# Feed-forward turns of a decoder kernel: where the square, the gelus, the table loads and the down projection stand

## The reference, cut to what matters

```
for i in range(6):
    x = attn_layer(shift_tokens(x), ...) + x
    x = ffn_layer(shift_tokens(x), ...) + x

attn_layer:  q, k, v = x @ Wqkv          # 16 heads of 64
             q, k = l2norm(q) * qs, l2norm(k) * ksc ; rotate both
             softmax(8 * q @ k.T, window of 32 and the one before) @ v @ Wo
ffn_layer:   xn = (x - mean) / sqrt(var + 1e-5) * g + bln
             a, gate = split(xn @ W1 + b1)                # 341 each
             (a * gelu(gate)) @ W2 + b2
```

## Time and profile before

| | before |
|---|---|
| runs (median, lowest, highest) | 1274.28 us, 1273.89, 1277.31 |
| the profiled execution | 1272.33 us, span of its trace 1270.5 us |
| the stack: first square sum L1680, last down pass L1375 | 397.8 us, 1254.7 us of the span |
| PE / DVE / ACT / POOL busy, whole span | 90% / 75% / 67% / 51% |
| head-norm square sum L1680 on POOL | 96 times, 1287 ns |
| squares L1426 on ACT | 192 times, 596 ns |
| square of the centred stream L1502 on ACT | 12 times, 613 ns |
| down projection L1375 on PE | 72 passes, 592 ns |
| table loads L1473, L1511, L1514 | 24, 12, 12 times, 1283 ns each |
| granted TensorE clock, 550 to 752 us | 1.00 of full speed |

### The profile page before, as it was taken

One profiled execution on the slowest core, in us unless ns is written; L12 is line 12 of the kernel. 1 busy time (PEld: TensorE's weight loads), 2 busy tenths in 40 slices (PEclk: granted clock), 3 DMA queues, 4 the chain that ended last, 5 costly groups with the idle time before them and its releaser, 6 DMA issues. The chain is left out here.

```text
span 1270.5 us, 26317 instructions
## 1 busy us (share of the span) xinstructions
PE 1138.3 (90%) x9636; PEld 720.2 (57%) x9636; DVE 949.0 (75%) x1399; ACT 847.5 (67%) x1356; POOL 650.1 (51%) x522
## 2 busy tenths in 40 slices
PE   7787869999765899999999999999999999999976
PEld 2222337777422576666656676666666666667541
DVE  2789957777465778787878788877878787878733
ACT  4553536665335588777877788678877787777844
POOL 1555723444323675664657465655566465756510
PEclk9888979999786899999999999999999999999997
DMA  3000007110200454344525453435434453534310
GB/s 113 1 1 0 1 17 217 51 50 1 77 24 19 97 155 99 93 123 107 133 74 129 103 134 88 112 102 134 99 98 123 109 126 76 126 90 120 87 49 17
DMA packets 75510, 107.11 MB, mean 84 GB/s; under 512 B 25347, under 2 KB 31938, under 8 KB 75002
## 3 DMA queue, kind: packets, MB, share of 16 engines
q1 hardware_dynamic: 75386, 105.47, 31.9%
HBM read 30.89 MB, written 0.59 MB: 25 GB/s over the span
## 5 line engine op out<-in xcount | busy, mean ns | idle before, releaser
L1680 POOL TENSOR_TENSOR st_sq_sum<-h 128x512 f32<-128x512 f32 x96 | 123.5, 1287 | 250.0 <-ACT h L1426 249.4
L1563 DVE SCALAR_TENSOR_TENSOR st_turned<-banks,mo_w 128x1024 f32<-128x1024 f32 x96 | 117.6, 1225 | 74.6 <-ACT banks L1437 43.2
L1426 ACT ACTIVATE h<-banks 128x512 f32<-128x512 f32 x192 | 112.1, 596 | 68.2 <-PE banks L1269 64.9
L1684 POOL TENSOR_TENSOR mo_w<-mo_w,x 128x512 f32<-128x512 f32 x96 | 122.5, 1276 | 61.4 <-DVE x L1549 60.5
L1330 PEld LDWEIGHTS banks<-st_p_blocks,st_vs 128*64 128x64 f32 x1536 | 81.8, 138 | 78.6 <-issue 74.6
L1289 PEld LDWEIGHTS banks<-st_wv,stream 128*128 128x128 f32 x768 | 100.6, 191 | 45.4 <-issue 44.7
L1686 POOL TENSOR_TENSOR mo_w<-mo_w,x 128x512 f32<-128x512 f32 x96 | 122.4, 1275 | 0.0
L1277 PE MATMUL banks<-st_sq_sum,head_ones 128*128 128x512 f32 x192 | 103.3, 620 | 16.1 <-POOL st_sq_sum L1680 16.1
L1458 ACT ACTIVATE st_p_blocks<-banks 64x512 f32<-64x512 f32 x192 | 112.2, 584 | 3.2 <-PE banks L1318 0.8
L430 POOL TENSOR_TENSOR ma_dbx<-ma_u,ma_b_rows 128x1024 f32<-128x1024 f32 x32 | 75.4, 2360 | 75.8 <-ACT ma_b_rows L288 51.9
L1693 POOL TENSOR_TENSOR mo_w<-st_prob,st_ri 128x512 f32<-128x512 f32 x96 | 100.2, 1044 | 15.2 <-DVE st_ri L1651 15.2
(11 more groups left out here) (234 smaller groups left out, 2780.1 us busy)
## 6 DMA issues: line engine op xcount, KB each, us to landing
st_qT<-st_turned SPq DMA_DIRECT2D x192, 128.0 KB, 2.4
st_k_blocks<-st_turned SPq DMA_DIRECT2D x384, 64.0 KB, 2.0
st_vs<-st_vn SPq DMA_DIRECT2D x96, 192.0 KB, 2.5
st_w_raw<-in_w_qk SPq DMA_DIRECT2D x12, 512.0 KB, 4.7
st_vs<-st_vn SPq DMA_DIRECT2D x96, 48.0 KB, 2.1
mo_w_all<-gate_rows SPq DMA_DIRECT2D x1, 3072.0 KB, 12.9
st_wv<-in_w_v SPq DMA_DIRECT2D x12, 256.0 KB, 3.0
st_wo<-in_wo SPq DMA_DIRECT2D x12, 256.0 KB, 3.0
```

Of the source, the lines that this page charges most:

```text
L1426: A(sq[:, part, :], ps[:, part, :], ACT.Square).then_inc(sq_done.sem, 1)
L1563: v.scalar_tensor_tensor(turned[:, h % 4], NORM_BANK.unsqueeze(1).to_broadcast([P, 2, SEQ]), 1e12, cos_part[:, which], ALU.min, ALU.mult). ...
L1680: nc.gpsimd.tensor_tensor(sq_sum[:], sq[:, 0, :], sq[:, 1, :], ALU.add).then_inc(sq_summed.sem, 1)
L1684: nc.gpsimd.tensor_tensor(cos_part[:, which, 0, :], cos_part[:, which, 0, :], sin_part[:, 1, :], ALU.subtract).then_inc(add_done.sem, 1)
```

## The change

Four things move within the four feed-forward stages; nothing is added or taken away but the place of the table loads.

1. Stage 0, ScalarE: the square of the centred stream comes right after `copy_probs`, ahead of `copy_v`, `logarithm` and `root`.
2. Stages 1 and 2, ScalarE: gelu's table load and the first gelu (stage 1) or the third (stage 2) come ahead of `copy_out`; the second gelu stays behind it.
3. Table loads: gelu's is now asked for by name after `root`. The load back moves from the end of stages 1 and 2 into the next turn, behind its two squares and ahead of its exponential.
4. Stage 3, TensorE: `down` comes ahead of `head_norm`.

```diff
--- before.py
+++ after.py
@@ -1398,12 +1398,12 @@
                     project_v(s, t + 1, job, stage)
                 if t >= -2 and s.unit(t + 2):
                     masks(s, t + 2)
+                if stage == 3:
+                    down(s, job)
                 if s.unit(t + 4):
                     head_norm(s, t + 4)
                 if stage in (1, 2):
                     up_gate(s, t, job, 0 if stage == 1 else 2)
-                if stage == 3:
-                    down(s, job)
                 if s.unit(t) and t >= 0:
                     values(s, t)
                 if stage == 0:
@@ -1484,34 +1484,35 @@
                     A(rstd[:], rstd[:], ACT.Exp, scale=-0.5).then_inc(rstd_step.sem, 1)
                 if s.unit(t + 4):
                     square(s, t + 4)
+                if stage in (2, 3):
+                    nc.scalar.preload_act_table_set("natural_log_exp_and_others")
                 if t >= -1 and s.unit(t + 1):
                     n = t + 1
                     ac.wait_ge(*sub_done.at(s.turn, n + 1))
                     A(prob[:, n % 2], prob[:, n % 2], ACT.Exp, scale=QK_SCALE).then_inc(exp_done.sem, 1)
                 if s.unit(t) and t >= 0:
                     copy_probs(s, t)
+                if stage == 0:
+                    ac.wait_ge(*centre_step.at(s.turn, 3 * job + 1))
+                    if stat_done.any(s.turn, 2 * job):
+                        ac.wait_ge(*stat_done.at(s.turn, 2 * job))
+                    A(dsq[:], dx[:], ACT.Square).then_inc(rstd_step.sem, 1)
                 if t >= -1 and s.unit(t + 1):
                     copy_v(s, t + 1)
                 if s.unit(t + 4):
                     logarithm(s, t + 4)
                     root(s, t + 4)
-                if stage == 0:
-                    ac.wait_ge(*centre_step.at(s.turn, 3 * job + 1))
-                    if stat_done.any(s.turn, 2 * job):
-                        ac.wait_ge(*stat_done.at(s.turn, 2 * job))
-                    A(dsq[:], dx[:], ACT.Square).then_inc(rstd_step.sem, 1)
+                if stage in (1, 2):
+                    nc.scalar.preload_act_table_set("gelu_and_others")
+                    if stage == 1:
+                        ac.wait_ge(*ffn_in.at(s.turn, 80 * (job + 1) if job < 1 else 80))
+                    gelu(s, job, 0 if stage == 1 else 2)
                 if t >= 0 and s.unit(t):
                     copy_out(s, t)
                 if 4 <= t < 8 and not s.last:
                     scale_table(s, (t - 4) // 2, t % 2, 1)
                 if stage == 1:
-                    ac.wait_ge(*ffn_in.at(s.turn, 80 * (job + 1) if job < 1 else 80))
-                    gelu(s, job, 0)
                     gelu(s, job, 1)
-                    nc.scalar.preload_act_table_set("natural_log_exp_and_others")
-                if stage == 2:
-                    gelu(s, job, 2)
-                    nc.scalar.preload_act_table_set("natural_log_exp_and_others")
                 if s.resplit(job, stage):
 
                     ac.wait_ge(*res2_done.at(s.turn, 2 * job + 2))
```

## The result

The changed kernel takes 1251.67 us (median of 4 runs, 1249.41 to 1253.78) against 1274.09 us of before (4 runs, 1267.6 to 1277.31): ratio of the runs 0.9832, 95% interval 0.9801 to 0.9863, so 1.7% faster. Timed again it was 0.9821 (0.9794 to 0.9848). The profiled execution took 1253.78 us, span 1252.0, that is 18.5 us less than before's 1272.33 and 1270.5; the sum of the prediction had 16.2.

A forecast was written before the change was run, and what follows sets the result against it. TensorE was taken to bound the feed-forward turns, except at hold-ups. Terms of 7.5, 6.5, 1.8 and 0.4 us sum to 16.2, taken from the median 1274.28 us: forecast 1258, eight-in-ten range 1253 to 1267.

The forecast's parts named there:

- What bounds the kernel: Feed-forward turns: TensorE is the bound except at hold-ups, such as 1.23 us before stage 0's variance and 0.57 in stage 3.
- the square: Stage 0, ScalarE: the centred stream's square moves ahead of three instructions, the variance starts sooner, 1.23 us handed to stage 1.
- Does stage 1 keep it?: Stage 1: GpSimd's sum may meet the cast or L1596; 0.2 us charged to each of five batch-0 jobs with casts.
- Load, gelu, copy out: Stages 1 and 2, ScalarE: reordering costs nothing by itself; squares come 1.3 us sooner, and stage 3's 0.57 us wait vanishes.
- Stage 3: Down before head norm: with stage 0's gain, next turn's product 1.37 us sooner by strict ends, up to 1.6; 1.5 taken.
- the chain: Stage 3, strict ends: down 2.68 us, then logarithm, root, copy out, y_high; 3.80 us from head norm to next turn's product.
- The sum: All jobs: 7.5 us for batch-1, 6.5 for batch-0 of layers 1 to 5, 1.8 and 0.4 for two last jobs; 16.2.
- The last job's term: Last job: the table load leaves the path ahead of the gelu that TensorE waits for, 0.4 us gained.
- A: Rival: the VectorE and GpSimd loop takes stage 0's gain, perhaps 0.3 us of it passes; 7.3 us gained, 1267; chance 0.13.
- B: Rival: all overlaps count and the loop speeds up, cast before sum; 1.75 us per job, 19.7 us, 1253.7; chance 0.09.
- C: Rival: sooner squares put GpSimd's sum on VectorE's stage 1 work (L1594, L1596); 9.8 us slower, 1284; chance 0.05.
- D: Rival: nothing moves; VectorE and GpSimd's loop uses up stage 0's gain, the root chain stage 3's 0.57 us; 1274; chance 0.05.

The follow-up runs named there:

- feed-forward load later: Changed kernel with only SyncE's load of the feed-forward weights one turn later (turn 6 instead of 5): 1250.41 us, ratio 0.9826.
- all three: Changed kernel with y_high between logarithm and root, stage 1's weight cast behind the rotation, feed-forward weights loaded one turn later: 1238.79 us, ratio 0.9754.
- all but down first: Changed kernel with head norm ahead of down again, as before the change: 1250.48 us, ratio 0.9833.
- the scaling first: Changed kernel with y_high sooner, feed-forward load later, and VectorE's scaling of the centred stream at the head of stage 1: 1242.24 us, ratio 0.9754.

## Why the prediction was right and wrong

**What bounds the kernel** and **the square** held. The variance starts as soon as TensorE comes to it, the copy out starts within 0.14 us of where it stood in its turn, and 1.30 us (1.23 predicted) go on to stage 1 in each of the eleven jobs.

**Does stage 1 keep it?** held in mechanism: the sum meets the cast in batch-0 jobs and L1596 in batch-1 jobs, which bear it. The size was off: 0.45 us lost instead of the 0.2 charged, since the cast is held for the whole sum and the multiplication follows it; four of the five batch-1 jobs even gain 0.13. The prediction had not seen that before the change GpSimd's sum was the one held in those jobs.

**Load, gelu, copy out** held: no other stage moves, and it takes away the wait in stage 3 by itself. The squares come 1.5 us sooner in stage 2 and 1.95 in stage 3, more than the one load of 1.3.

**Stage 3** is the step that failed, in its size. The prediction took 0.57 us of idle time from the row of the head norm and chained the rest by strict ends, 1.37 us a job together with stage 0, and chose 1.5. Less the 1.23 of stage 0 that is 0.14 by the chain and 0.27 as chosen. Measured: 0.85 won, 0.24 lost, so 0.61 in stage 3 and the turn after. With stages 0 and 1 it is 2.0 us in a typical batch-1 job and 1.5 in a batch-0 job. Three terms of the chain were off. Down starts 5.77 us into the turn (651.06 - 645.29) instead of 5.93 (653.92, with the scores at 649.22 - 1.23): the 0.57 us stand against the modelled end of the mask product, whose last 0.16 us lie behind the next start (0.38 long, next start 0.22 later where nothing waits). Down takes 653.64 - 651.06 = 2.58 us to the next start, not 2.68. And from the head norm's start to the next turn's product the prediction had 3.80 us, where the trace has 657.24 - 653.64 = 3.60. Together 0.46, and 0.14 + 0.46 = 0.60.

The 0.85 us alone comes out of the wait in this way: 0.57 + 0.16, and 0.10 because the head norm that had waited takes 0.96 us to the start of the next 512-column product instead of 0.86 in stage 1 of the same job, in all 0.83. A wait is worth the distance of starts with and without it, not the bracket.

**The sum, against the profile.** Predicted 5 x 1.5 + 5 x 1.3 + 1.8 + 0.4 = 16.2. Measured by turns: five batch-1 jobs 9.8, five batch-0 jobs 7.6, the last layer's batch-0 job 2.3 (it has no -0.24), the start of the stack 0.2 sooner, all other turns and the last job together 1.4 slower: 18.5. The term for stage 3 is the largest miss: ten jobs at 0.61 instead of 0.27, 3.4 us. The last job's term held: from its gate product to its value product it takes 3.54 or 3.55 us in all nine traces with the load ahead and 4.15 in the three without, so 0.6 us up to there where 0.4 was charged; the value products behind it take 2.2 to 2.9 us in the twelve traces and may give back a part. Its sum is hidden by the clock: in the changed kernel's trace the granted clock was 0.51 in its stage 0 and the mean product's two passes took 2.07 us; in before's they took 1.13, ahead of the fall to 0.60.

**The sum, against the runs.** The medians are 22.4 us apart, the traces 18.5. The other 4 us of the miss came from carrying an execution to a median: before's lies 1.8 us over its profiled execution, and the changed kernel's profiled execution was its slowest of four, 2.1 us over the median. The table shows where this scatter is: the first scores of the stack start up to 6 us sooner (feed-forward load later) or 1.5 us later (all three) than before's, in code that is the same in all of them. Nor do the 1.5 us lost in the other turns belong to the change, for the runs with a single edit lose 1.0 to 2.4 us there too, and all but down first loses none. What the change itself does is the first column and up to 0.6 us in the last job, 19.8 + 0.6 = 20.4 us. Both intervals cover it (17.5 to 25.4 us and 19.3 to 26.2 us); the 18.5 us of the two spans only the first does. With 20.4 instead of 16.2 the forecast would have been 1274.28 - 20.4 = 1253.9, just inside the range; the last 2 us to 1251.67 are within the scatter. So the miss of the range took both, the mis-sized stage 3 and a draw of runs that fell on the same side. How the scatter comes about before the stack stays open. The range should have held 5 us of it on top of the bounds of the sum.

**Rivals.** A fell with the run of the square alone. B was nearest, 19.7 us against 20.4, partly by luck: all overlaps count, but 2.0 us a job hold for the batch-1 jobs only and 1.5 for the others, for the cast did not get in before the sum. C's prices are real: 1.77 - 0.68 = 1.09 us on L1594 when the cast is away, 1.38 - 0.55 = 0.83 on L1596 in five batch-1 jobs (C counted six; the last has no sum beside it). On L1596 it doesn't decide, because VectorE has that slack. The rule of the Trainium skill, page SBUF — State Buffer, section on the two separate sides, that a VectorE instruction with two SBUF inputs and a GpSimd operation reading SBUF exclude each other, of which the trace before showed nothing, agrees with these traces in both directions: the multiplication is 1.09 us longer beside the sum, the sum 0.37 us beside the multiplication. Both are some 0.14 us less than a wait to the other's end would cost (1.22 us and 0.51 us), and GpSimd's spans are rough. D fell.

## What to carry to other kernels

When two edits remove the same wait, time them apart: here the gelus and table loads on one side and down first on the other each give 0.85 us a job, together still 0.85, and the second costs 0.24. Ask of every moved block what now stands last in front of the next stage's input; it was y_high behind logarithm, root and copy out, and moving that one instruction gave 8.1 us by turns. Size a stall by the starts around it in a turn that has it and in one that hasn't; compare traces turn by turn when the runs scatter by more than the effect, and take the change from the turns that it touches, not from the whole span.

## What the runs showed of the hardware that I had not expected

VectorE's plain float32 multiplication of two SBUF tiles, 0.68 us alone, took 1.77 us when GpSimd's addition had started 0.05 us before it. GpSimd's addition, 1.27 us alone, took 1.64 us when it started 0.17 us into such a multiplication, 1.27 when it started 0.53 us into it, and 1.49 to 1.55 us when it started 0.1 to 0.2 us into the scaling L1596 (before, and the run with the scaling first). A TensorE wait shown as 0.57 us idle was worth 0.85 us of the turn.
